# Two attention layers, a feed-forward layer and a mixture of experts on one core: probabilities of two query units turned together, values from a block-diagonal copy, evictions in pairs

## The reference, cut to what matters

```python
x = x + L0_ffn(L0_cond(x, ...), ...)
x = x + L1_ffn(L1_cond(x, ...), ...)

# attention of both layers, 16 heads of 64; one shared key and value head, and a null key and value
xn = ln(x); q = heads(xn @ Wq); k, v = split(xn @ Wkv)
k, v = concat([nk, k]), concat([nv, v])
q, k = l2norm(q) * q_scale, l2norm(k) * k_scale      # layer 0 alone
sim = q @ k.T * scale + bias                          # relative in layer 0, given in layer 1
attn = softmax(where(causal & mask, sim, -max))
out = ln((attn @ v) @ Wout) * g_out
# L0_ffn: layer norm, ternary weights 128x512, gelu, layer norm, ternary weights 512x128
# L1_ffn: 8 experts, the two best of each token, capacity 320, relu
```

## Time and profile before

| | us |
|---|---|
| profiled execution | 678.2 |
| its span, first to last instruction | 676.4 |
| median of the runs | 679.29 |
| TensorE busy | 532.8 (79%) |
| VectorE busy | 453.9 (67%) |
| ScalarE busy | 395.6 (58%) |
| GpSimd busy | 326.2 (48%) |

### The profile page before, as it was taken

The page is one execution under the profiler, slowest core; times in us unless marked ns, Lnnn a source line. Parts: engine busy times, 40 slices in busy tenths (PEclk is TensorE's granted clock), DMA queues, the critical chain, the costliest instruction groups (busy, mean ns, idle before and its releaser), DMA issues.

```text
span 676.4 us, 14426 instructions
## 1 busy us (share of the span) xinstructions
PE 532.8 (79%) x3433; PEld 389.6 (58%) x3433; DVE 453.9 (67%) x2254; ACT 395.6 (58%) x1505; POOL 326.2 (48%) x389
## 2 busy tenths in 40 slices
PE   1058899999999997895799989999898704999930
PEld 0035566666666655665667767767675503887830
DVE  2647899999999987463767887887877531344223
ACT  1038788878878885762667777777667201345310
POOL 4234676575566572655423432432247661354560
PEclk9998999999999999996989999999899765999985
DMA  3823950000000000000000000000001112344216
GB/s 107 213 55 91 202 137 0 0 0 0 0 0 0 1 1 1 1 1 0 1 1 2 0 0 0 0 0 0 2 6 40 43 38 55 100 122 123 83 39 190
DMA packets 42493, 28.04 MB, mean 41 GB/s; under 512 B 8729, under 2 KB 38866, under 8 KB 42450
## 3 DMA queue, kind: packets, MB, share of 16 engines
q1 hardware_dynamic: 39890, 22.66, 14.1%
q0 software_dynamic: 2560, 4.90, 2.2%
HBM read 16.13 MB, written 11.42 MB: 41 GB/s over the span
## 4 chain that ended last, share of the span: by engine, by line
PE 36%; DVE 9%; issue 7%; POOL 6%; DMA 4%; ACT 1%; SPq 1%; DVEq 0%; POOLq 0%; ACTq 0%
PE psS L776 6%; PE psA L813 5%; PE psS L1010 5%; PE psO L794 4%; POOL wide_buf L581 3%; PE psQ L1000 3%; PE psT L785 3%; PE psQ L749 3%; DVE sc L1368 2%; DMA slot_rows<-Y,dest_u 2%; PE psQ L941 2%; PE psO L1000 1%; PE psA L1000 1%; DVE OT L1389 1%; POOL slot_rows L593 1%
## 5 line engine op out<-in xcount | busy, mean ns | idle before, releaser
L1092 ACT ACTIVATE sc<-sc,negmax 128x97 f32<-128x97 f32 (+3 forms) x512 | 178.9, 356 | 12.4 <-DVE negmax L1368 10.3
L1100 ACT COPY PT<-psT 32x512 f32<-32x512 f32 (+3 forms) x128 | 73.7, 576 | 83.2 <-PE psT L785 77.4
L776 PE MATMUL psS<-kk,qT 128*128 128x194 f32 (+3 forms) x512 | 106.0, 328 | 17.4 <-DVE negmax L1368 12.4
L581 POOL TENSOR_TENSOR wide_buf<-bias,mask 128x132 f32<-128x132 f32 (+3 forms) x128 | 105.6, 850 | 6.5 <-DVE negmax L1368 4.1
L776 PEld LDWEIGHTS psS<-kk,qT 128*128 128x128 f32 x512 | 75.9, 190 | 54.7 <-issue 51.4
L1368 DVE CUSTOM_DVE_ANT_0 sc<-psS,wide_buf 128x97 f32<-128x97 f32 (+3 forms) x512 | 93.2, 238 | 20.7 <-PE psS L776 16.1
L1092 ACT ACTIVATION_READ_ACCUMULATOR sc<-sc,negmax 128x1 f32 x512 | 98.5, 192 | 0.0
L794 PE MATMUL psO<-PT,vp 96*64 96x256 f32 (+3 forms) x512 | 84.7, 408 | 9.6 <-DVE OT L1389 7.1
L785 PE MATMUL psT<-ident,pn 128*96 128x128 f32 (+3 forms) x512 | 78.5, 276 | 7.0 <-issue 5.9
L529 POOL TENSOR_TENSOR qrn<-qssc,half 128x9 f32<-128x9 f32 (+1 forms) x32 | 55.0, 1736 | 56.5 <-DVE qssc L1354 56.5
L1379 DVE TENSOR_TENSOR pn<-sc,rsum 128x128 f32<-128x128 f32 (+3 forms) x128 | 74.1, 579 | 7.6
(11 more groups left out here) (242 smaller groups left out, 937.3 us busy)
## 6 DMA issues: line engine op xcount, KB each, us to landing
eW<-in_L_ffn_W SPq DMA_DIRECT2D x16, 256.0 KB
slot_rows<-empty SPq DMA_DIRECT2D x2, 1390.0 KB, 12.5
xb<-slot_rows SPq DMA_DIRECT2D x16, 139.0 KB
choice_rows<-zero_row SPq DMA_DIRECT2D x8, 256.0 KB, 8.0
wide_buf<-choice_rows SPq DMA_DIRECT2D x8, 256.0 KB, 4.8
Wq<-in_L_cond_Wq SPq DMA_DIRECT2D x2, 512.0 KB, 6.9
out_x<-X SPq DMA_DIRECT2D x4, 256.0 KB, 3.7
xb<-slot_rows SPq DMA_DIRECT2D x16, 34.8 KB
```

The source lines that it names most:

```text
L581: pool.tensor_tensor(unit_masked(i, u).rearrange("p h e k -> p (h e) k"), unit_bias(layer, u).rearrange("p h e k -> p (h e) k"), mask[laye ...
L776: m = pe.matmul(psS[:, h, 0:2 * w], qT[i][:, h, u].rearrange("p m q -> p (m q)"), kk[i][:, :, 0:w], start=True, stop=True)
L1092: m = act.activation(v, v, ACT.Exp, bias=negmax[:, u, g:g + 1], scale=-1.0, accum_out=psum_row[:, u, g:g + 1])
L1100: act.copy(PT[u % 2][0:k].rearrange("p h e q -> p (h e q)"), psT[0:k, u % 2, :]).then_inc(s["probsT_ready"], 1)
```

## The change

- The probabilities of units 0 and 1 are turned together (`turn_pair`): one transpose for the four groups of 32 keys of unit 0, two for the groups of 64 keys of unit 1. Units 2 and 3 are turned as before. pn has a buffer per unit.
- The turned probabilities of the pair then lie with their groups one below another on the partitions. So the values need block-diagonal operands, vp_u0 (32-row blocks) and vp_u1 (64-row blocks), zero elsewhere. `spread_values` on SyncE copies vp into them with six small DMAs per batch, in SyncE's program after the experts' weights.
- `values_pair` makes two products of 128 columns and one of 256; `values` does units 2 and 3 in one go. psO is now used whole, and `outputs` evicts 512 columns twice per batch in place of 256 four times.
- The floor under the sums of squares moves from VectorE to GpSimd, ahead of each power.
- In layer 0 the output norm no longer divides by its own deviation: `out_centred` writes the centred row times g_out straight from psA, and carries (variance + eps) * eps in hvs. The statistics of the feed-forward's input are made in groups of four tiles (`dense_stats`, `dense_rstd`), two groups in the last batch, one behind the last evictions, one behind the gate's copy; the root there counts hvs in.

```diff
+            def spread_values(layer):
+                def batch(b, i):
+                    B = b + NB * layer
+                    sp.wait_ge(s["v_ready"], B + 1)
+                    for g in range(4):
+                        sp.dma_start(vp_u0[i][QB * g:QB * (g + 1), g // 2, DH * (g % 2):DH * (g % 2 + 1)],
+                                     vp[i][0:QB, :]).then_inc(s[f"vp_in{i}"], 16)
+                    for e in range(2):
+                        sp.dma_start(vp_u1[i][DH * e:DH * (e + 1), DH * e:DH * (e + 1)],
+                                     vp[i][0:DH, :]).then_inc(s[f"vp_in{i}"], 16)
+
+                over(sp, NB, batch)
+
+            spread_values(0)
+            spread_values(1)
...
             def q_norm(b):
 
                 for h, (lo, hi) in enumerate(((0, 9), (9, HEADS + 1))):
-                    pool.wait_ge(s["ss_step"], 4 * b + 2 * h + 2)
+                    apart(pool, (s["ss_step"], 2 * b + h + 1))
+                    pool.tensor_scalar(qssc[:, lo:hi], qss[:, lo:hi], 1e-24, None, ALU.max).then_inc(s["q_floor"], 1)
+                    pool.wait_ge(s["q_floor"], 2 * b + h + 1)
                     rsqrt(qrn[:, lo:hi], qssc[:, lo:hi], hi - lo, s["rn_ready"])
...
-                held(pool, s["out_psum"], 4 * B - 4)
+                held(pool, s["out_psum"], 2 * B - 2)
...
-                    if not (no(b, 0) or no(b, 1)):
-                        output_rstd(b - 2 + NB * layer, i)
-                    if layer == 0 and not (no(b, 0) or no(b, 1) or no(b, 2)):
-                        input_rstd("h", b - 3, b - 3, 1 - i)
+                    if layer == 1 and not (no(b, 0) or no(b, 1)):
+                        output_rstd(b - 2, i)
...
-            def turn_probs(n, u):
-
-                apart(pe, (s["probs_ready"], n + 1), (s["probsT_ready"], n - 1))
+            def turn_pair(B, i):
+
+                apart(pe, (s["probs_ready"], 4 * B + 2), (s["probsT_ready"], 3 * B - 1))
+                pe.transpose(psT[:, i, 0:P], pn[0][:].rearrange("p g k -> p (g k)"), ident[:])
+                for h in range(2):
+                    m = pe.transpose(psT[:, i, (h + 1) * P:(h + 2) * P],
+                                     pn[1][:, 2 * h:2 * h + 2, :].rearrange("p e k -> p (e k)"), ident[:])
+                m.then_inc(s["probsT_psum"], 1)
+
+            def turn_probs(B, u, i):
+
+                apart(pe, (s["probs_ready"], 4 * B + u + 1), (s["probsT_ready"], 3 * B + u - 2))
                 k = WIDTH[u] - 1
                 for g in range(4):
-                    m = pe.transpose(psT[0:k, u % 2, g * P:(g + 1) * P], pn[u % 2][:, g, 0:k], ident[:])
+                    m = pe.transpose(psT[0:k, probs_bank(u, i), g * P:(g + 1) * P], pn[u][:, g, :], ident[:])
                 m.then_inc(s["probsT_psum"], 1)
 
-            def values(n, u, i, B=None):
-
-                apart(pe, (s["probsT_ready"], n + 1), (s["out_ready"], n),
-                      *([(s["v_ready"], B + 1)] if u == 0 else []))
-                k = WIDTH[u] - 1
-                for e in range(2):
-                    m = pe.matmul(psO[DH * e:DH * (e + 1), 0:256], vp[i][0:k, :], PT[u % 2][0:k, :, e, :],
-                                  start=True, stop=True)
+            def values_pair(B, i):
+
+                apart(pe, (s["probsT_ready"], 3 * B + 1), (s["out_ready"], 2 * B),
+                      (s[f"vp_in{i}"], arrived(B, i, 96)))
+                for h in range(2):
+                    pe.matmul(psO[:, h * P:(h + 1) * P], vp_u0[i][:, h, :], PT[0][:, 0:P], start=True, stop=True)
+                pe.matmul(psO[:, 2 * P:4 * P], vp_u1[i][:], PT[0][:, P:3 * P], start=True, stop=True).then_inc(
+                    s["out_psum"], 1)
...
+            def values(B, i):
+
+                apart(pe, (s["probsT_ready"], 3 * B + 3), (s["out_ready"], 2 * B + 1), (s["v_ready"], B + 1))
+                for u in (2, 3):
+                    k = WIDTH[u] - 1
+                    for e in range(2):
+                        m = pe.matmul(psO[DH * e:DH * (e + 1), 2 * P * (u - 2):2 * P * (u - 1)], vp[i][0:k, :],
+                                      PT[u - 1][0:k, :, e, :], start=True, stop=True)
                 m.then_inc(s["out_psum"], 1)
...
-                    n = 4 * (b + NB * layer)
+                    B = b + NB * layer
                     first, last = no(b, 0), no(b, NB - 1)
-
-                    def earlier(u, lag):
-
-                        return not (first and u < lag)
 
                     for u in range(UNITS):
                         scores(layer, b, u, i)
-                        if earlier(u, 2):
-                            turn_probs(n + u - 2, (u - 2) % UNITS)
+                        if u < 2 and not first:
+                            turn_probs(B - 1, u + 2, 1 - i)
                         if u == 0 and not last:
                             project_in(layer, b + 1, 1 - i)
+                        if u == 1 and not first:
+                            values_pair(B - 1, 1 - i)
+                        if u == 3:
+                            turn_pair(B, i)
                         if u == 3 and not last and not no(b, NB - 2):
                             turn_input(layer, b + 2, i)
-                        if earlier(u, 3):
-                            values(n + u - 3, (u - 3) % UNITS, i if u == 3 else 1 - i, b + NB * layer)
+                        if u == 3 and not first:
+                            values(B - 1, 1 - i)
...
-            def weights_T(n, u):
-                act.wait_ge(s["probsT_psum"], n + 1)
-                held(act, s["out_psum"], n - 1)
+            def pair_T(B, i):
+                act.wait_ge(s["probsT_psum"], 3 * B + 1)
+                held(act, s["out_psum"], 2 * B - 1)
+                act.copy(PT[0][:], psT[:, i, 0:3 * P]).then_inc(s["probsT_ready"], 1)
+
+            def weights_T(B, u, i):
+                act.wait_ge(s["probsT_psum"], 3 * B + u)
+                held(act, s["out_psum"], 2 * B)
                 k = WIDTH[u] - 1
-                act.copy(PT[u % 2][0:k].rearrange("p h e q -> p (h e q)"), psT[0:k, u % 2, :]).then_inc(
+                act.copy(PT[u - 1][0:k].rearrange("p h e q -> p (h e q)"), psT[0:k, probs_bank(u, i), :]).then_inc(
                     s["probsT_ready"], 1)
...
-                dve.wait_ge(s["ss_step"], 4 * b + 2 * h + 1)
-                dve.tensor_scalar(qssc[:, lo:hi], qss[:, lo:hi], 1e-24, None, ALU.max).then_inc(s["ss_step"], 1)
...
-            def outputs(layer, n, b, u, i):
-                B = b + NB * layer
-                dve.wait_ge(s["out_psum"], n + 1)
-                if u == 0:
+            def outputs(B, half_of, i):
+                dve.wait_ge(s["out_psum"], 2 * B + half_of + 1)
+                if half_of == 0:
                     held(dve, s["y_psum"], B - 1)
-                dve.tensor_scalar(OT[i][:, :, u, :], psO[:, 0:256].rearrange("p (j q) -> p j q", q=QB),
+                dve.tensor_scalar(OT[i][:, :, 2 * half_of:2 * half_of + 2, :],
+                                  psO[:].rearrange("p (u j q) -> p j u q", u=2, q=QB),
                                   cols[:, C_VN:C_VN + 1], None, ALU.add).then_inc(s["out_ready"], 1)
...
+            def out_centred(b, i):
+
+
+                apart(dve, (s["o_stat"], 2 * b + 1))
+                dve.bn_aggr(o_mv[:, i, :], o_st[:, i, :]).then_inc(s["o_stat"], 1)
                 if no(b, 0):
                     dve.wait_ge(late_in, 16 * LATE_DMAS)
-                dve.wait_ge(s["o_rstd"], b + NB * layer + 1)
-                if layer == 1:
-                    dve.scalar_tensor_tensor(centred[:, P:P + EXPERTS], gate_sum[:], run["o"][1][:, i, 0:1],
-                                             Y[:, b, RAW_AT:RAW_AT + EXPERTS], ALU.mult, ALU.subtract)
-                dve.scalar_tensor_tensor(centred[:, 0:P], Y[:, b, 0:P], run["o"][1][:, i, 0:1], g_out[layer][:],
+                apart(dve, (s["o_stat"], 2 * b + 2))
+                dve.scalar_tensor_tensor(Y[:, b, 0:P], psA[:, Y_AT[0]:Y_AT[0] + P],
+                                         o_mv[:, i, 0:1], g_out[0][:],
+                                         ALU.subtract, ALU.mult).then_inc(s["y_done"], 1)
+                dve.tensor_scalar(hvs[:, bass.ds(b, 1)], o_mv[:, i, 1:2], LN_EPS, LN_EPS, ALU.add,
+                                  ALU.mult).then_inc(s["o_small"], 1)
+
...
+            def dense_stats(g):
+
+                quad = slice(4 * g, 4 * g + 4)
+                dve.wait_ge(s["y_done"], 4 * g + 4)
+                for t in range(4 * g, 4 * g + 4):
+                    ins = dve.bn_stats(stats[:, t, :], Y[:, t, 0:P])
+                step(ins)
+                for t in range(4 * g, 4 * g + 4):
+                    ins = dve.bn_aggr(mv[:, t, :], stats[:, t, :])
+                step(ins)
+                dve.wait_ge(s["o_small"], 4 * g + 4)
+                dve.tensor_tensor(hve[:, quad], hvs[:, quad], mv[:, quad, 1], ALU.add).then_inc(s["h_var"], 1)
...
```

(18 more changed lines are left out.)

242 lines of the change are left out of this document (128 added, 114 removed).

## The result

The changed kernel takes 698.03 us (median of four runs, 694.81 to 699.74), the kernel before 680.88 (four, 677.43 to 685.59): a ratio of 1.0236, 95% interval 1.0196 to 1.0276. It is slower, by 2.4%; whether by more than 2%, the interval leaves open. The profiled executions have spans of 697.9 and 676.4 us.

A forecast was written before the change was run, and what follows sets the result against it. It took layer 0 as bound by a ring through ScalarE, VectorE and TensorE, layer 1 by TensorE plus a 0.62 us wait. Terms +26 +1 +1 -19 = +9 on 678.2 gave 687, 688 as median; range 672 to 701.

The forecast's parts named there:

- The small DMAs, +26: Layer 0's start: first small DMAs queue behind expert weights on SyncE, blocking TensorE 28 us; +26 us, bounds 23 and 30.
- Layer 1, -19: Layer 1's batches: period falls from 12.47 to TensorE's own work, 11.1 us; -19 us, bounds 10 and 24.
- the 0.8: TensorE work saved per batch in both layers: about 0.6 us from fewer transposes, 0.2 from values.
- Rival 2: Layer 1: GpSimd's block still ends last, so only 10 us instead of 19 is gained; 697 us, chance 0.13.
- Layer 0, +1: Layer 0's settled batches: a ring through three engines keeps the period at 13.2 to 13.3 us; +1, ends -3 and +7.
- The ends of layer 0, +1: Norms at layer 0's ends: grouped statistics and an extra power against fewer waits for GpSimd; +1 us, ends -3 and +4.
- Rival 1: Layer 0: TensorE's clock falls because of 1.2 us idle before kd per batch; 696 us, chance 0.2.

The follow-up runs named there:

- the kernel before with its block held back: Kernel before, with GpSimd's block of four bias additions in layer 1 waiting until VectorE has read the scores of unit 1: 676.14 us.
- Four orders of the same work: Layer 0 as in the change (698.03 us), then three successive reorderings with small DMAs early: 678.76, 673.61 and, with both edits of layer 1, 652.31 us.
- the norm part alone: Kernel before plus GpSimd floors, shortened output norm, grouped statistics and VectorE's new order; no paired turning, small DMAs or wider evictions: 682.03 us.
- The kernel that the experiments point to: The change with small DMAs early, layer 1's key copies early and GpSimd block held back, layer 0 reordered, output norm and input copy later still: 652.31 us.
- both edits of layer 1: The change with small DMAs early, layer 1's key and value copies ahead of unit 1's work, and GpSimd's bias block held back: 659.81 us.

## Why the prediction was wrong

The forecast was 688, 9 us slower, and "within 2%" the likeliest; the measured 698 lies in the range, but 17 us above the kernel before. The profiled executions lie 21.5 us apart: the gain of layer 1 was 9 us too high, the stall 5 us too dear, and the rest, 8.6 us, was underrated or not in the sum. By its own steps, in the profiled executions:

- **The small DMAs, +26.** Right in place, mechanism and releaser; the size is 20 to 21 (19.8 by the medians, 20.9 in the second batch), below the least it allowed, 23. TensorE came to the wait at 70.1 and not 66.5, because its second batch started 3.2 us later; the first DMAs landed at 92.3 and not 94.5; a wait of 22.24 delayed the third batch by 20.9, so the work done meanwhile gave back 1.3 us net of the low clock, where the forecast has 1.5 (2.5 less 1). That part was right; the wait was too long by 6.
- **Layer 1, -19: this is the step that failed.** It was -9.9, just under the least gain it allowed, 10. "So the period should fall to TensorE's own work, 12.47 - 0.62 - 0.8 = 11.1 us" puts every wait but one at nothing and has two errors that hide each other. The first is the 0.8: with the marked waits gone in both, the period differs by 1.84 us. The turnings save 0.7, near the 0.6 of the forecast, but the values 0.85 and not 0.2 (about half of it short waits that no row marks), and the scores and projections some 0.3. The second is that taking the wait before values out left two that had been covered by it and by the work behind it: 11.79 less 10.13, 1.66 us per batch. VectorE, still held by GpSimd's block, is late with the biased scores of unit 1 for TensorE's scores of unit 2; I had looked at the eviction alone, which the change moves away from there. Behind those scores the turning of unit 0 and the values of unit 3 had stood, 1.3 us (431.41 to 432.71 in the rows of the kernel before with its block held back), and they covered all but 0.2 us of ScalarE's key copy; the change takes them away and the projection waits.
- **Rival 2** named the first of these waits ("scores of unit 2 still need the bias additions past it") with 10 us instead of 19. That price is right by luck: it keeps the 0.8 and no second wait. Its trigger, a block that starts later, did not happen: it starts 1.4 us into the batch (458.19 to 459.57), before 1.65. Its total of 697 is close by luck too, with a stall 5 us cheaper and 5 us outside the sum.
- **Layer 0, +1.** +1.0 in ten periods (132.9 against 131.9), +1.8 in the twelve from the third batch on; kd 4.72 after the sums against 4.65 to 4.7, the floor 0.25 against 0.2 to 0.3. So the term was right, but in part by luck, since the two halves of the change pull apart: the norm part alone costs 0.3 us per batch, and with the rest of the change 0.2 of it come back. Nor is kd the one link that binds: with kd 1.45 us earlier the period stayed. Four orders of the same work gave 13.29, 13.28, 13.11 and 12.98, each time with another wait. Which set of links would have to be shortened together for a period near 12 is open; three expectations of mine on it failed, and a fourth, on the norm part alone, had the period 0.1 us too short.
- **The ends of layer 0, +1.** Measured +0.2 and +3.3, within the bounds of -3 to +4. The stretch from the last batch's start to the first feed-forward product takes 21.69 us before and 23.48 after, 20.57 with the norm part alone. So the norm part gained 1.1 there, and the rest of the change, which has the last values and evictions in pairs, cost 2.9; which of its parts, no run shows. The other 1.5 us, in the feed-forward layer itself, are not explained.
- **Not in the sum:** 1.1 us before the first batch, 2.1 in it and 2.1 behind the attention. Parts of these are TensorE at half speed, whose place moves from kernel to kernel: from 52 to 56 us TensorE had a granted clock of 0.56 after the change and 1.00 (51 to 56 us) before, and the first batch takes from 13.01 to 13.97 us in the four kernels that have the small DMAs early and layer 0 as the change has it; the kernel before with its block held back has a dip at 266 to 274 us, in code that it shares with the kernel before, and takes 24.30 us there in place of 21.69. They can't be put down to the change one by one.
- Rival 1, the clock inside layer 0: wrong, it stayed at full there with 1.2 to 1.3 us idle before kd in each batch.

The Trainium skill, "SBUF — State Buffer" (section "SBUF: two separate sides"), says that VectorE and GpSimd share one pair of ports, which a VectorE instruction needs when it has two inputs in SBUF or runs in a mode that uses two ports; that the pair is locked for a whole instruction, and that the loser blocks fully. The traces agree: `centred` and xn took 0.34 us each without the block beside them, with it `centred` took 1.29 us, and xn started 0.07 us behind its end.

The kernel that the experiments point to takes 652 us against 681, a ratio of 0.9572 (0.9535 to 0.9610). Not all of that is the change's: the kernel before gains from the held block too (676.14), and it was not run with the other moves. With the block held in both, and the key copies early in the changed one, it is 659.81 against 676.14, each beside its own 681 or 682. So the change was worth having; what spoiled it was one place in one queue, and in layer 1 two waits, one removed by moving two calls, the other by two added lines.

## What to carry to other kernels

A new DMA's cost is its place in the queue that issues it: read what stands ahead of it at the first time it is needed, not only in the settled loop. When work is taken out of a full engine, list every wait that this work covered, and price the period without any wait by a run rather than by the wait that one row shows. Where two waits stand in one batch, as here in layer 1, removing either may gain only part and lengthen the other (0.66 and 0.60 us alone, 1.65 together). In a ring over several engines a shorter link need not shorten the period: in layer 0 kd came 1.45 us sooner for nothing, and four orders lie about 0.3 us apart at most.

## What the runs showed of the hardware

- The releaser that a row names can be the wrong one of two that end close together: the projection's row names VectorE's eviction (written by 465.50), and moving ScalarE's key copy (written by 465.45) removed the wait; the projection then started 0.49 us before that eviction ended.
- GpSimd's additions held VectorE's division of 256 columns too: it took 1.30 us beside them in layer 0 (190.48, after) and 0.42 in layer 1 without them (466.34). Not each time: with both edits of layer 1 it took 1.27 us beside the block in one batch and 0.43 in the next, where the block took 3.28 us in place of 2.99.
- A wait too short to be marked can still be read: in the kernel before with its block held back the projection starts 0.14 us behind the key copy, and the values ahead of it seem to take 0.77 us instead of 0.58.
- TensorE fell to half speed right behind waits of 1.14 and 1.07 us, 0.3 us of work between, in the second batch of layer 0 (the last rows of the experiments), but stayed at full in the settled batches of layer 0 after the change, each of which holds a wait of 1.2 to 1.3 us. What tells the two apart the runs do not show.
